# T

## The chip

a

## The reference

b

## The kernel before

c

## Time and profile before

d

### The profile page before, as it was taken

How to read it: one execution, taken by the hardware profiler on the slowest of the kernel's cores; microseconds unless marked ns; L12 is line 12 of the kernel's file. 1: busy time of each engine (PE TensorE's matmuls, PEld its weight loads, DVE VectorE, ACT ScalarE, POOL GpSimd, SP SyncE). 2: the span in 40 equal slices, each digit the busy share in tenths (PEclk: the TensorE clock that was granted, in tenths of full speed). 3: DMA queues.
4: the chain of work that ended last, by engine and by line, in shares of the span. 5: the costliest groups of instructions: out<-in, count | busy, mean ns of one | idle time of the engine just before them, and what ended most of it. 6: DMA issues, size and time to landing. Idle time of an engine off the chain costs nothing.

```text
span 3754.5 us, 41907 instructions; the slowest of 8 cores (3702.6 to 3754.5 us)
## 1 busy us (share of the span) xinstructions
PE 2815.8 (75%) x12672; PEld 1093.2 (29%) x12672; DVE 1725.6 (46%) x2582; ACT 752.6 (20%) x1317; POOL 292.3 (8%) x540
## 2 busy tenths in 40 slices
PE   0001787789977989689967988698869897899676
PEld 0000221323332333223322333233323333343222
DVE  2221555363645444463636454545455454736312
ACT  0000220304022220404022401322041304140201
POOL 0111000001000110001000110011000100110010
PEclk9999665879987899979987999789987999999878
DMA  6886000202230223213240233123321323122222
GB/s 197 241 242 172 12 4 20 62 23 71 85 101 29 57 82 88 75 31 89 67 112 17 63 96 87 48 57 85 96 68 40 92 78 90 52 84 73 90 79 84
DMA packets 108706, 303.98 MB, mean 81 GB/s; under 512 B 16192, under 2 KB 24768, under 8 KB 108496
## 3 DMA queue, kind: packets, MB, share of 16 engines
q1 hardware_dynamic: 61520, 169.14, 15.7%
q0 software_dynamic: 46976, 132.15, 12.6%
q8 instruction: 118, 1.93, 0.2%
q14 instruction: 92, 0.75, 0.1%
HBM read 269.77 MB, written 39.85 MB: 82 GB/s over the span
## 4 chain that ended last, share of the span: by engine, by line
PE 59%; DVE 12%; DMA 9%; issue 6%; ACT 4%; DVEq 0%; SPq 0%; ACTq 0%; POOLq 0%; POOL 0%
PE P L709 9%; PE P L440 9%; PE P L397 9%; PE P L387 8%; PE P L725 8%; PE P L622 6%; PE P L563 3%; DVE p_sb L674 3%; DMA wgb<-wg_s 3%; DMA wub<-wu_s 2%; PE P L763 2%; DMA wob<-wout_s 2%; DVE esum L648 2%; DMA wqb<-wq_s 2%; PE P L338 2%
## 5 line engine op out<-in xcount | busy, mean ns | idle before, releaser
L674 DVE TENSOR_TENSOR p_sb<-P,vdup 128x512 bf16<-128x512 f32 x1024 | 698.3, 689 | 387.5 <-PE P L725 351.2
L387 PE MATMUL P<-x_bf,wgb 128*128 128x512 bf16 x1536 | 526.4, 411 | 106.5 <-DMA wub<-wu_s 88.8
L709 PE MATMUL P<-e_sb,selz_sb 16*128 16x512 bf16 x1024 | 456.2, 455 | 130.9 <-DVE e_sb L658 77.3
L397 PE MATMUL P<-x_bf,wub 128*128 128x512 bf16 x1536 | 536.2, 409 | 7.4 <-DVE h_sb L413 7.3
L725 PE MATMUL P<-p_sb,id_sb 128*128 128x256 bf16 x2048 | 514.4, 317 | 35.1 <-DVE p_sb L674 31.2
L597 DVE TENSOR_TENSOR hadb<-q_sb,krep 128x2048 bf16<-128x2048 bf16 x256 | 309.9, 1224 | 470.1 <-PE P L622 310.2
L440 PE MATMUL P<-h_sb,wdb 128*128 128x512 bf16 x1536 | 481.9, 390 | 15.2 <-DVE r_bf L449 14.2
L622 PE MATMUL P<-hadb,selred_sb 128*16 128x256 bf16 x2048 | 324.5, 276 | 45.5 <-DVE hadb L597 21.4
L406 ACT ACTIVATE s_sil<-P 128x512 bf16<-128x512 f32 x192 | 114.4, 596 | 1052.0 <-PE P L387 1045.6
L305 PE MATMUL P<-x_bf,wd_sb 128*128 128x512 bf16 x128 | 35.4, 419 | 355.8 <-DMA x_bf<-xt 355.7
L763 PE MATMUL P<-avn,wob 128*128 128x256 bf16 x1024 | 249.5, 289 | 43.0 <-DMA wob<-wout_s 30.5
L413 DVE TENSOR_TENSOR h_sb<-s_sil,P 128x512 bf16<-128x512 bf16 x192 | 130.4, 679 | 305.4 <-PE P L397 230.8
L725 PEld LDWEIGHTS P<-p_sb,id_sb 128*128 128x128 bf16 x2048 | 170.5, 102 | 266.3 <-issue 232.8
L387 PEld LDWEIGHTS P<-x_bf,wgb 128*128 128x128 bf16 x1536 | 146.2, 101 | 317.8 <-issue 246.1
L709 PEld LDWEIGHTS P<-e_sb,selz_sb 16*128 16x128 bf16 x1024 | 91.9, 93 | 502.7 <-issue 502.7
L256 POOL DMA_DIRECT2D wgb<-wg_s x192 | 104.9, 547 | 1674.9 <-PE P L397 1674.2
L397 PEld LDWEIGHTS P<-x_bf,wub 128*128 128x128 bf16 x1536 | 153.5, 102 | 220.5 <-issue 134.0
L622 PEld LDWEIGHTS P<-hadb,selred_sb 128*16 128x16 bf16 x2048 | 153.4, 89 | 215.9 <-issue 192.5
L440 PEld LDWEIGHTS P<-h_sb,wdb 128*128 128x128 bf16 x1536 | 146.9, 99 | 203.0 <-issue 97.8
L338 PE MATMUL P<-x_bf,wqb 128*128 128x512 bf16 x512 | 138.2, 426 | 87.0 <-DMA wqb<-wq_s 75.7
L774 DVE SCALAR_TENSOR_TENSOR r_bf<-P,bout_sb,x_bf 128x256 bf16<-128x256 f32 x128 | 61.6, 482 | 246.6 <-PE P L763 246.6
L217 DVE CAST stgb<-stg 128x1024 bf16<-128x1024 int32 (+1 forms) x88 | 61.0, 694 | 226.2 <-DMA wg_s<-stgb 56.8
(65 smaller groups left out, 1933.0 us busy)
## 6 DMA issues: line engine op xcount, KB each, us to landing
wdb<-wdn_s SPq DMA_DIRECT2D x64, 768.0 KB, 4.5
wgb<-wg_s POOLq DMA_DIRECT2D x192, 256.0 KB, 3.0
wub<-wu_s POOLq DMA_DIRECT2D x192, 256.0 KB, 3.0
wob<-wout_s SPq DMA_DIRECT2D x128, 256.0 KB, 3.0
wqb<-wq_s SPq DMA_DIRECT2D x64, 256.0 KB, 3.0
yt<-x2b SPq DMA_DIRECT2D x64, 256.0 KB, 2.1
stg<-wg SPq DMA_DIRECT2D x24, 512.0 KB, 5.3
stg<-wu SPq DMA_DIRECT2D x24, 512.0 KB, 5.2
```

The source lines that it names most:

```text
L338: e.matmul(o, l, r, start=st, stop=sp)),
L387: e.matmul(o, l, r, start=st, stop=sp)),
L397: e.matmul(o, l, r, start=st, stop=sp)),
L406: e.activation(o, i, AF.Silu, scale=1.0 / 127.0)),
L413: h_v.append(add('V', (lambda e, o=o, a=a, b=b: e.tensor_mul(o, a, b)), waits=w, inc=s_v2, d=780))
L440: e.matmul(o, l, r, start=st, stop=sp)),
L597: add('V', (lambda e, o=o, a=q3, b=b: e.tensor_mul(o, a, b)), waits=tuple(w), inc=s_v, d=1460)
L622: e.matmul(o, l, r, start=st, stop=sp)),
L674: add('V', (lambda e, o=o, a=a, b=b: e.tensor_mul(o, a, b)), waits=w, inc=s_v, d=640)
L709: e.matmul(o, l, r, start=True, stop=True)),
L725: e.matmul(o, id_sb[:, :], r, start=st, stop=sp)),
L763: e.matmul(o, l, r, start=st, stop=sp)),
```

## The change

e

## Rows read from the trace of the kernel before

**Rows 1.** The page's first part, busy time by engine.
```profile
span 3754.5 us, 41907 instructions; the slowest of 8 cores (3702.6 to 3754.5 us)
...
PE 2815.8 (75%) x12672; PEld 1093.2 (29%) x12672; DVE 1725.6 (46%) x2582; ACT 752.6 (20%) x1317; POOL 292.3 (8%) x540
```

**Rows 2.** Windows, the six seams behind steps 1 to 6.
```profile
sum 129.00, PE 92.34 PEld 33.66 DVE 42.32 ACT 62.29 POOL 25.88; mean PE 15.39 PEld 5.61 DVE 7.05 ACT 10.38 POOL 4.31
```

**Rows 3.** Timeline behind step 5, and windows behind steps 5, 0 and 7.
```profile
2708.17 5.13 PE L440 MATMUL P<-h_sb,wdb 128*128 128x512 bf16 x23
...
2718.14 0.60 ACT L463 ACTIVATE musq<-P 128x512 f32<-128x512 f32 x1 [0.67 <-PE P L504]
...
2719.82 1.28 ACT L466 ACT_TABLE_LOAD   x1 [1.08 <-DVE vpe L472]
2721.12 0.72 ACT L466 ACTIVATE lnscr<-vpe,cvec_sb 128x512 f32<-128x512 f32 x1
...
2723.50 0.59 PE L846 MATMUL P<-r_bf,ones_sb 128*128 128x512 bf16 x1 [5.51 <-DVE nmb L477]
...
2723.50:2729.10 5.60, 5.30 (x17) 1.79 (x17) 4.77 (x7) 3.56 (x6) 0.00 (x0) 0.76 0.25 94
691.10:699.50 8.40, 5.81 (x18) 1.84 (x17) 4.93 (x8) 2.63 (x4) 1.08 (x2) 0.80 0.45 63
3502.90:3523.40 20.50, 4.97 (x18) 1.56 (x15) 17.21 (x28) 5.51 (x9) 0.00 (x0) 0.67 0.20 77
```

**Rows 4.** Windows, q projection of step 1, then steps 2 to 7.
```profile
700.50:720.20 19.70, 17.07 (x69) 6.71 (x70) 6.63 (x10) 4.81 (x7) 0.00 (x0) 0.90 0.37 107
...
sum 180.90, PE 108.28 PEld 40.30 DVE 96.01 ACT 28.86 POOL 0.00; mean PE 18.05 PEld 6.72 DVE 16.00 ACT 4.81 POOL 0.00
```

**Rows 5.** Timeline of step 3's q projection, SP's queue and PE.
```profile
1544.05 0.32 SPq L256 DMA_DIRECT2D wqb<-wq_s  x1
...
1552.77 0.58 PE L338 MATMUL P<-x_bf,wqb 128*128 128x512 bf16 x1 [5.89 <-DMA wqb<-wq_s]
```

**Rows 6.** Windows of AV0 (steps 5, 1 to 6, 7, 0), a block, and AV1.
```profile
2413.90:2497.60 83.70, 76.77 (x275) 22.41 (x276) 51.30 (x83) 2.98 (x5) 5.50 (x11) 0.72 0.12 32
...
sum 503.00, PE 460.82 PEld 136.53 DVE 308.46 ACT 17.91 POOL 32.86; mean PE 76.80 PEld 22.75 DVE 51.41 ACT 2.98 POOL 5.48
...
3209.90:3288.20 78.30, 75.08 (x330) 26.83 (x331) 53.98 (x87) 4.78 (x8) 9.84 (x18) 0.97 0.21 58
435.30:512.00 76.70, 66.48 (x186) 13.73 (x186) 48.24 (x77) 0.00 (x0) 0.00 (x0) 0.50 0.00 1
...
2447.10:2461.70 14.60, 14.52 (x43) 4.09 (x42) 6.50 (x10) 0.60 (x1) 1.09 (x2) 0.56 0.13 36
...
sum 474.80, PE 457.50 PEld 161.24 DVE 308.65 ACT 18.30 POOL 26.23; mean PE 76.25 PEld 26.87 DVE 51.44 ACT 3.05 POOL 4.37
```

**Rows 7.** Groups by line, and who waited for s_sil (us, times).
```profile
L709 PE MATMUL P<-e_sb,selz_sb 16*128 16x512 bf16 x1024 | 456.2, 455 | 130.9 <-DVE e_sb L658 77.3
...
L597 DVE TENSOR_TENSOR hadb<-q_sb,krep 128x2048 bf16<-128x2048 bf16 x256 | 309.9, 1224 | 470.1 <-PE P L622 310.2
...
L305 PE MATMUL P<-x_bf,wd_sb 128*128 128x512 bf16 x128 | 35.4, 419 | 355.8 <-DMA x_bf<-xt 355.7
...
  PE P L387: 1.3, 5
```

**Rows 8.** Windows, WO1 of step 0, then steps 1 to 6.
```profile
666.80:685.50 18.70, 13.59 (x65) 8.33 (x66) 3.38 (x7) 1.26 (x2) 0.00 (x0) 0.59 0.39 109
...
sum 157.30, PE 132.92 PEld 73.54 DVE 31.66 ACT 7.56 POOL 0.00; mean PE 22.15 PEld 12.26 DVE 5.28 ACT 1.26 POOL 0.00
```

**Rows 9.** Windows, WO0 and the stretch behind it, step 5.
```profile
2565.40:2601.90 36.50, 28.70 (x160) 14.89 (x160) 16.20 (x34) 4.87 (x7) 6.06 (x12) 1.00 0.51 144
```

**Rows 10.** Timeline of PE, first gate matmuls of the last FFN.
```profile
3523.37 3.15 PE L387 MATMUL P<-x_bf,wgb 128*128 128x512 bf16 x7 [15.03 <-DVE x2b L492]
```

More of the change, by code:

```diff
@@ L403, in plan_ffn_ch2 @@
                     w.append((s_v2, v0 + m - 1))
[L404 removed]
+                o, i_ = s_sil[m % 2][:, :], P[0 if m % 2 == 0 else 4][:, :]
                 add('S', (lambda e, o=o, i=i_:
@@ new lines, in plan_ffn_ch2 @@
+            for J in range(XC):
+                w = [(s_s2, sc2 + J + 1)]
+                if J == 0:
+                    w.append((s_s, ck['musq1']))
+                o2, r2 = P[3][:, :], sqb2[J % 2][:, :]
+                add('T', (lambda e, o=o2, r=r2, st=(J == 0), sp=(J == XC - 1):
+                          e.matmul(o, ones_sb[:, :], r, start=st, stop=sp)),
+                    waits=w, inc=s_pe2)
+            ex2_val = add('S', (lambda e, o=vpe2[:, :], i=P[3][:, :]:
+                                e.activation(o, i, AF.Identity,
+                                             scale=1.0 / 1024.0)),
+                          waits=[(s_pe2, pe2 + XC), (s_v2, ck['vpesub2'])],
+                          inc=s_s2)
```

208 lines of the change are left out of this document (122 added, 86 removed).

## The prediction

> **What bounds the kernel now.** I read the page's first part, then cut the span into the phases of a main step with the windows view, then the timeline at the places where PE stands still. PE is busy 75% of a 3754.5 us span and no other engine passes half [rows 1]; the first 345 us are weight preparation, which the change leaves alone. After that come eight steps of 512 tokens, and beside the attention of step s runs the feed-forward network (FFN) of step s-1, at places that the planner fixes when the program is built. So the question is not how busy PE is, but what each phase waits for.
>
> Between the last output-projection matmul of a step and the first head matmul of the next (the seam) lie 129.0 us over six steps, 21.5 each [rows 2]. In it PE does 23 left-over w_down matmuls, both LayerNorm statistics in turn, and stands 5.51 us in between, because the second statistics share P3 and P4 with the first and wait for nmb2 [rows 3]. The q projection behind it takes 180.9 us over steps 2 to 7, 30.2 each, and 19.7 in step 1, where no output is stored [rows 4]: SP issues in order, and by its order wqb loads stand behind yt stores that wait for x2b, and the last one behind two wdb loads, three times its size each, so that PE waits up to 5.89 us for one load, 8.7 us after its issue [rows 5]. The first attention-value phase of a step (AV0) takes 503.0 us over steps 1 to 6, 83.8 each, in step 5 at a mean granted clock of 0.72; in step 7 it takes 78.3 at 0.97 although it holds 150 FFN matmuls by the order and not 92, and in step 0 it takes 76.7 with none, at 0.50, the lower of the two levels, 1.2 GHz [rows 6]. So this phase is not limited by PE's work but by the ring PE, DVE, PE through two banks; FFN matmuls ride in it nearly free.
>
> **The change part by part.** The sum is made against the profiled execution, 3756.1 us. That is 0.85% above the median, 3724.24, so the result is scaled by 0.9915 at the end.
>
> The direct gains are small. The second gate bank P4 removes a wait of PE for the SiLU that is 1.3 us in the whole run, and the second x buffer a wait for x of 355.8 less the first 346.3, some 9.4 us, nearly all in step 1 [rows 7]. What counts is that the shorter dependences change the planner's order, as the rows of the order show, and that order is what I cost.
>
> Seam, steps 1 to 6. The w_down tail and all of the second LayerNorm's 16 matmuls move ahead of the end of the output projection. The seam is left with eight squares against ACT in lockstep, bounded by the old block of 16 (5.6 us [rows 3]; the pace is ACT's, so half the matmuls save nothing); then the eviction of E[x2] with Ln2 and its table load queued ahead of it on ACT, 1.28+0.72+0.60=2.6; then eight mean matmuls, 8 x 0.22=1.8 (0.22 is 5.13/23). Sum 10.0: 6 x 10=60 against 129.0, **-69**. Ends: 8 (if ACT reaches the eviction early) and 14 each, -81 to -45.
>
> Here a rule of the Trainium skill speaks against the change. Our rows have Ln starting 1.30 us after its table load begins [rows 3]. The page "ScalarE: Activation LUTs", section "What ACT_TABLE_LOAD costs", gives 1283 ns for the load and some 1380 ns more for a drain. By it a seam would be 1.4 us longer, some 8 us over six. The trace agrees on the load and shows no drain, so none is in the sum.
>
> q projection. SP's new order has all of wqb behind at most two yt, whose x2b is made before the head ends; the wdb pair stands behind. Six phases at 19.7 plus 1 us for the first gate matmul (below) are 124.2 against 180.9, **-57**. Ends: 19.7 gives -63; if half of the excess stays, -31.
>
> AV0. It now holds 139 FFN matmuls, 13 in the first of its eight blocks and 17 to 19 in the others, where before the first two blocks held 0 to 4. Its nearest row is step 7's 78.3. The one block in which the clock recovers under FFN work takes 14.6 instead of 9.6, an eighth of 76.7 [rows 6], and may now fall at the start. I take 80: 6 x 80=480 against 503.0, **-23**. Ends: 78.3, -33, and two such blocks on top of it, 88.3, +27.
>
> Second output projection (WO1), 157.3 over steps 1 to 6 [rows 8], 26.2 each, and I count step 7 the same, 183.5 in all. It holds 40 w_down matmuls and the 16 of the second statistics, not 87. Its first half stays at 3.2 us per group of 8; the second half is held by wob loads, 18.7/8=2.3 per group in step 0, where nothing else is there [rows 8]. 4 x 3.2+4 x 2.3=22, taken as 22.5, 157.5 over seven: **-26**. Ends: 18.7 each (-53) and no gain.
>
> First output projection with the stretch behind it, 36.5 us [rows 9], is held by the gate and up loads (95 gate and up matmuls, six pairs of loads). It now has 98 and five more of w_down: +1 each, **+7**, ends 0 and +18. AV1 loses 48 gate and up matmuls and gets 42 w_down; its 474.8 over six steps, 79.1 each [rows 6], stays.
>
> Seam behind step 0: statistics 5.6 become 8.1 (no Ln2 there), the head's 8.4 with its x waits [rows 3] become 3.6: **-2**.
>
> Last seam. Before, the first gate matmul of the last FFN starts 20.5 us behind WO1 and waits 15.03 us for the last x2b [rows 10]. It still has to, and the second LayerNorm's outputs are now begun only behind Ln2: nmb2 at about 8 us, then 32 DVE operations up to that x2b, at 28 in 20.5 us as before [rows 3], 23.4: 31.5, taken as 32.5, **+12**; ends 0 and +16. The last FFN itself keeps its loads and their order. Tail: means behind squares add an eviction, 8 matmuls and one more ACT pass, each with a hand-over: 0.9+1.9+0.9, **+4**, ends +2 and +5.
>
> -69-57-23-26+7-2+12+4=-154. 3756.1-154=3602, times 0.9915 is **3572 us**.
>
> **The rivals.** *The clock stays low in AV0 (slower).* PE still stands ahead of AV0 for the normalised e_sb [rows 7], and the 0.72 of today's phase says that its first half runs at the lower level. At that level 17 FFN matmuls of twice 0.22 on a ring of 9.6 make a block of up to 17; the one row for it, 14.6, had the clock back before its end [rows 6]. At 16 a phase is 128, +44 on the old one and +265 over six, against -131 from the other terms: 3890, scaled 3857. It decides where a phase passes 105.6 (+21.8), that is, from four or five such blocks of eight on. Against it: in step 5 the block behind the 14.6 is part of a phase that ends at full speed, and step 7 runs at 0.97. 6%.
>
> *The wait is only moved (no change).* The first gate matmul stands in PE's queue among the key and value projections, and needs the last x2b. I put that x2b at 41 us behind WO1: nmb2 at 9, then 34 DVE operations of 0.75 and two had of 1.22 [rows 7], and 4 for yt stores that have to land. PE comes there at 39 to 44: seam 10, head 4.7, q 20.6, key/value matmuls 4 to 9. If yt stores and had operations push it 15 us further, PE stands with everything behind it: +90, so -64, scaled 3661. 8%.
>
> *Only the direct waits go.* If phases are held by things that the reordering doesn't touch, 9.4+1.3=11 us stay: 3713. Against it: the q phase's excess is there by cause [rows 4, 5]. 6%.
>
> **How the numbers follow.** The forecast has 80%. A timing of this kernel can tell about 2% from no change, so faster means below 3650. All the good ends together give some -230, all the bad ones about -10, and neither is likely: I take -196 to -75, 3530 to 3650. What is left out below is the good ends, above the rivals. Faster 0.80, within 2% 0.15 (the second and third rival, and a little of the first), slower 0.05.
>
> **What would show it.** In the changed kernel's profile: seams of about 10 us; no PE wait over 3 us for wqb and q phases near 20; AV0 near 80 at a clock over 0.9; WO1 near 22; the last FFN starting some 32 us behind WO1; one Ln table load in front of L840's eviction. Wrong would be: AV0 above 90, PE waits of over 5 us at L395 for an x2b in every step, or a seam that is still 20 us.

## The result, and the profile after

The change takes the kernel from 3725.6 to **3674.6 us** (medians of 6 and 7 runs), a ratio of **0.9858** with a 95% interval of 0.9839 to 0.9878: 1.4% faster, clear of noise but below the 2% from which the prediction counted a change as faster. The forecast was 3572 us with a range of 3530 to 3650. The direction was right, the size was not: 51 us of the 152 that it forecast. In some runs of any of these kernels one die shows a lower granted clock and the time is up to some per cent longer; medians are over all runs, ratios and intervals over the others alone.

The sections ahead of the prediction on the chip, the reference, the kernel before, its time and the change hold single letters in place of text. The description stands at the end of this document, under "The kernel and the change", and was not on record with the prediction; a reader who is new to the kernel should take it first.

The page of the changed kernel (its first part and the row of the granted clock, in tenths per fortieth of the span):

```profile
span 3671.2 us, 41956 instructions; the slowest of 8 cores (3639.1 to 3671.2 us)
...
PE 2758.6 (75%) x12672; PEld 1090.5 (30%) x12672; DVE 1725.1 (47%) x2582; ACT 774.0 (21%) x1349; POOL 292.5 (8%) x540
...
PEclk9999756689998999999989999998999998999778
```

The profiled execution took 3673.0 us, within 0.05% of the median. That of before was 0.85% above the median of its first two runs. The views of the cores, before and then after, show why: before, one die had a lower granted clock than the other, and the slowest core, of which every row ahead of the prediction is one, lies on it.

```profile
core 0: 3754.5 us, clock 0.880
die 0 (median of its cores): 3746.3 us, clock 0.884
die 1 (median of its cores): 3712.4 us, clock 0.898
```

```profile
core 7: 3671.2 us, clock 0.901
die 0 (median of its cores): 3648.1 us, clock 0.909
die 1 (median of its cores): 3663.9 us, clock 0.903
```

The clock records of the traces say what the lower mean is made of. Beside 1.00 (2.4 GHz) and 0.50 (1.2 GHz) they hold stretches at a granted 0.81: 235 to 274 us in all on each of cores 0 to 3 of before and none on its cores 4 to 7; none in x_two_old_order (below), and in the changed kernel 27 to 59 us on each of cores 4 to 7 alone.

So core 0 of before is a poor base for the phases in which the clock matters. For the balance I use the mean of eight cores, and as base a kernel that differs from before only in having two x buffers under the same order (x_two_old_order, below: ratio 1.0012), whose execution shows no such die.

The windows that answer to [rows 2], [rows 4], [rows 6] and [rows 8], slowest core of the changed kernel, cut at the same matmuls: the six seams, q of steps 2 to 7, AV0, WO1 and AV1 of steps 1 to 6:

```profile
sum 62.50, PE 38.89 PEld 12.18 DVE 16.90 ACT 45.27 POOL 3.23; mean PE 6.48 PEld 2.03 DVE 2.82 ACT 7.55 POOL 0.54
...
sum 129.80, PE 94.70 PEld 36.24 DVE 89.49 ACT 28.95 POOL 0.00; mean PE 15.78 PEld 6.04 DVE 14.92 ACT 4.82 POOL 0.00
...
sum 484.50, PE 446.69 PEld 158.66 DVE 321.06 ACT 28.71 POOL 52.44; mean PE 74.45 PEld 26.44 DVE 53.51 ACT 4.78 POOL 8.74
...
sum 142.90, PE 123.58 PEld 68.04 DVE 28.07 ACT 34.23 POOL 18.35; mean PE 20.60 PEld 11.34 DVE 4.68 ACT 5.71 POOL 3.06
...
sum 483.10, PE 460.70 PEld 160.34 DVE 301.46 ACT 7.58 POOL 10.20; mean PE 76.78 PEld 26.72 DVE 50.24 ACT 1.26 POOL 1.70
```

The seams fall from 129.0 to 62.5 (10.4 each, forecast 10.0), q from 180.9 to 129.8 (forecast 124.2). WO1 goes from 157.3 to 142.9, AV0 from 503.0 to 484.5, and AV1 rises from 474.8 to 483.1.

In this table a phase lasts from its first matmul to the first of the next, summed over the eight steps and averaged over the eight cores of one execution each, in us. "Last" is all behind the last WO1.

| phase | base | x_two | stats_one_bank | gate_one_bank | changed | before_costs | combined |
|---|---|---|---|---|---|---|---|
| seams | 133 | 51 | 133 | 72 | 70 | 66 | 72 |
| head | 50 | 51 | 54 | 55 | 55 | 54 | 55 |
| q | 223 | 209 | 164 | 168 | 170 | 198 | 164 |
| KV0 and SC0 | 323 | 322 | 330 | 327 | 327 | 324 | 329 |
| gap ahead of AV0 | 75 | 75 | 75 | 75 | 75 | 75 | 75 |
| AV0 | 665 | 667 | 673 | 671 | 671 | 699 | 644 |
| KV1 and SC1 | 499 | 509 | 507 | 502 | 501 | 493 | 499 |
| WO0 and the stretch behind | 297 | 312 | 304 | 326 | 326 | 298 | 283 |
| AV1 | 644 | 649 | 687 | 632 | 657 | 702 | 635 |
| WO1 | 197 | 183 | 190 | 185 | 184 | 186 | 181 |
| last | 252 | 256 | 266 | 267 | 272 | 268 | 207 |
| span, with what lies ahead of step 0 | 3704 | 3628 | 3726 | 3623 | 3655 | 3706 | 3489 |
| median of the runs | 3727.9 | 3651.7 | 3753.9 | 3644.1 | 3674.6 | 3726.0 | 3503.4 |

(before_costs is not quite the changed kernel at the old costs; see there.)

The changed kernel wins 115 us in the seams and q, and 13 in WO1. It gives back 29 in WO0 and the stretch behind it, 14 in AV1, 6 in AV0, 20 behind the last WO1 and 10 in small pieces. That makes -49, and the medians say -51.

### The profile page after: what moved, and what is told of

Read it like the earlier page. It is cut to its first block, busy times and chain, and to the rows that moved or that the text cites. A ratio compares the mean times of both kernels' runs of the same rounds, so it can differ in the third digit from the quotient of the medians.

```text
span 3671.2 us, 41956 instructions; the slowest of 8 cores (3639.1 to 3671.2 us)
## 1 busy us (share of the span) xinstructions
PE 2758.6 (75%) x12672; PEld 1090.5 (30%) x12672; DVE 1725.1 (47%) x2582; ACT 774.0 (21%) x1349; POOL 292.5 (8%) x540
## 4 chain that ended last, share of the span: by engine, by line
PE 60%; DVE 9%; DMA 9%; issue 6%; ACT 4%; DVEq 0%; ACTq 0%; POOLq 0%; SPq 0%; POOL 0%
PE P L448 10%; PE P L405 9%; PE P L731 9%; PE P L395 9%; PE P L747 8%; PE P L644 7%; PE P L585 3%; DVE p_sb L696 3%; DMA wgb<-wg_s 3%; DMA wub<-wu_s 3%; PE P L344 2%; PE P L785 2%; DVE esum L670 2%; DMA wqb<-wq_s 2%; DMA wob<-wout_s 1%
## 5 line engine op out<-in xcount | busy, mean ns | idle before, releaser
L395 PE MATMUL P<-x_bf,wgb 128*128 128x512 bf16 x1536 | 519.9, 407 | 110.5 <-DMA wub<-wu_s 90.2
L405 PE MATMUL P<-x_bf,wub 128*128 128x512 bf16 x1536 | 518.2, 406 | 19.1 <-DVE h_sb L421 19.1
L731 PE MATMUL P<-e_sb,selz_sb 16*128 16x512 bf16 x1024 | 427.9, 425 | 131.7 <-DVE e_sb L680 68.5
L448 PE MATMUL P<-h_sb,wdb 128*128 128x512 bf16 x1536 | 504.9, 393 | 17.1 <-DVE r_bf L457 16.4
L747 PE MATMUL P<-p_sb,id_sb 128*128 128x256 bf16 x2048 | 496.4, 300 | 23.9 <-DVE p_sb L696 17.7
L644 PE MATMUL P<-hadb,selred_sb 128*16 128x256 bf16 x2048 | 321.8, 276 | 43.0 <-DVE hadb L619 20.4
L311 PE MATMUL P<-x_bf,wd_sb 128*128 128x512 bf16 x128 | 36.4, 434 | 354.1 <-DMA x_bf<-xt 353.9
L785 PE MATMUL P<-avn,wob 128*128 128x256 bf16 x1024 | 235.1, 292 | 43.4 <-DMA wob<-wout_s 29.0
L747 PEld LDWEIGHTS P<-p_sb,id_sb 128*128 128x128 bf16 x2048 | 177.7, 101 | 223.4 <-issue 173.4
L395 PEld LDWEIGHTS P<-x_bf,wgb 128*128 128x128 bf16 x1536 | 150.8, 102 | 307.7 <-issue 225.8
L731 PEld LDWEIGHTS P<-e_sb,selz_sb 16*128 16x128 bf16 x1024 | 91.9, 92 | 489.4 <-issue 488.4
L261 POOL DMA_DIRECT2D wgb<-wg_s x192 | 104.9, 546 | 1558.4 <-PE P L405 1550.6
L405 PEld LDWEIGHTS P<-x_bf,wub 128*128 128x128 bf16 x1536 | 150.6, 102 | 222.5 <-issue 138.6
L644 PEld LDWEIGHTS P<-hadb,selred_sb 128*16 128x16 bf16 x2048 | 151.8, 89 | 211.8 <-issue 189.0
L448 PEld LDWEIGHTS P<-h_sb,wdb 128*128 128x128 bf16 x1536 | 144.0, 99 | 213.6 <-issue 126.3
L344 PE MATMUL P<-x_bf,wqb 128*128 128x512 bf16 x512 | 127.3, 400 | 53.9 <-DMA wqb<-wq_s 38.3
```

What stands on the lines that cost most here:

```text
L344: e.matmul(o, l, r, start=st, stop=sp)),
L395: e.matmul(o, l, r, start=st, stop=sp)),
L405: e.matmul(o, l, r, start=st, stop=sp)),
L448: e.matmul(o, l, r, start=st, stop=sp)),
L644: e.matmul(o, l, r, start=st, stop=sp)),
L731: e.matmul(o, l, r, start=True, stop=True)),
```

## The experiments

They ran in four groups, each with runs of the kernel before on the same chip. First, the parts of the change, alone and left out.

**x_two_old_order.** The kernel before with the two x buffers. The waits of before stay visible to the planner and are not carried out (`pw`), so every engine's order is the old one.

```diff
+                if c == 0 and ck['kv_pe_end']:
+                    pw.append((s_pe, ck['kv_pe_end']))
+                pw.append((s_v, max(ck['wo0_list'][c], ck['wo1_list'][c])))
+                w.append((s_v, ck['wo_free'][s % 2][c]))
...
-            for sem, val in nd[0]:
+            for sem, val in nd[0] + PW[id(nd)]:
```

> The kernel before with two x buffers, the planner still seeing the old waits, so that every engine's order is that of before. If the change works through the order (theory 'order'), only the x waits go, nearly all in step 1: -5 to -10 us of 3725, and the seams stay at 21.5 and q at 30. If the removed wait itself matters (theory 'direct waits'), -30 us or more and head or q phases shorter in every step.

3727.9 us, ratio 1.0012 (0.9998 to 1.0026). The buffer by itself is worth nothing that the time shows. The q phases keep their 223 us, and the head loses 5 (55 in before, by the same mean over eight cores).

**x_two.** The same buffers, with the planner seeing the new waits.

> The same two x buffers, now seen by the planner. By the order it moves 47 FFN matmuls into AV0 and leaves 41 w_down matmuls in WO1 and none in the seam; LayerNorm statistics stay on two banks in turn. Theory 'order': seam down from 21.5 to about 15, AV0 at 84 with 139 FFN matmuls, total 3685 to 3705. Theory 'direct waits': the same time as with the old order, within 5 us.

3651.7 us, ratio 0.9803 (0.9785 to 0.9821). The same buffer gives 76 us once the order may change, more than either theory said. Its seams are 51 us in the table, 7 each, although both LayerNorms still take P3 and P4 in turn: the order alone puts the w_down tail and the second LayerNorm ahead. The forecast had named the sharing of P3 and P4 as what holds the seam, and had not split the gain between the parts of the change. This one part is also faster than the whole change (0.9803 against 0.9858, intervals apart).

**stats_one_bank.** The changed kernel with one x buffer and gate on P0: only the statistics and the costs.

```diff
-        x_bf = [E(nc.sbuf_tensor(f"x_bf{i}", ...)) for i in range(2)]
+        x_bf = [E(nc.sbuf_tensor("x_bf", [128, XC * ST], BF16))] * 2
...
+                if c == 0 and ck['kv_pe_end']:
+                    w.append((s_pe, ck['kv_pe_end']))
-                wfree = ck['wo_free'][s % 2]
+                wfree = ck['wo_free'][0]
```

> The changed kernel with one x buffer and gate on P0 alone: the LayerNorm statistics on one bank and the stated costs are all that is left of the change. Theory 'the statistics carry it': seams near 11 and q near 22, so -100 us there, and part of it is given back in WO0 and AV1, in all 3670 to 3690, as good as the whole change. Theory 'x carries it': 3700 or more, with seams at 16 or above.

3753.9 us, ratio 1.0073 (1.0047 to 1.0100): slower than before. Seams stay at 133, q falls to 164, and AV1 rises to 687; in this order it holds 40 gate and up and 119 w_down matmuls. The second theory held: without the second x buffer there is no gain in the seams or in the time. But q falls by 59 us with one x buffer, so q's gain comes with the statistics and the costs, which no run here tells apart.

**gate_one_bank.** The changed kernel with gate on P0 alone.

```diff
-                    w.append((s_s2, sc0 + m - 1))
+                    w.append((s_s2, sc0 + m))
-                    o = P[0 if m % 2 == 0 else 4][:, :]
+                    o = P[0][:, :]
```

> The changed kernel with gate on P0 alone. Its order has the same numbers of FFN matmuls by phase as the changed kernel. The wait for SiLU was 1.3 us in the whole run before, so 3675 within 8 us if the second gate bank is worth nothing; 3690 or more if DVE and ACT hold PE in gate groups now that more of them lie in AV0.

3644.1 us, ratio 0.9777 (0.9754 to 0.9799): the second gate bank makes the change 30 us worse. By the table it is AV1, 632 against 657; everything else is within 6 us. **gate_two_banks_one_bank_order** asks whether it is the bank or its order: gate on P0 and P4, SiLU waits for the group before visible to the planner alone.

> The changed kernel with gate on P0 and P4 as it stands, but every engine's order that of gate_one_bank (the planner sees the wait for the SiLU of the group before). If the 30 us between gate_one_bank (3644) and the changed kernel (3675) are the order's, this takes 3635 to 3655 and AV1 is at 632 per core, not 657. If the second bank itself costs (theory 'bank'), 3670 or more.

AV1 is at 633.5 us per core, and the mean core took 3616 us, against 3623 for gate_one_bank and 3655 for the changed kernel. So the profile puts it on the order. Of its four runs (3639.7, 3663.7, 3671.9 and 3690.7 us) only the first can enter a ratio; it lies in the 3635 to 3655 expected, but one run has no interval, and by the times alone the question would stay open.

**before_costs.** This was meant as the changed kernel with the planner's costs as they were (700 for Square, 510 for x1). Its edit does more: it also raises the cost of the 1024 products `p_sb` of the AV blocks, which is 640 in both kernels, to 830.

```diff
-                    waits=w, inc=s_s2, d=850)
+                    waits=w, inc=s_s2)
...
-                            waits=w, inc=s_v, d=640)
+                            waits=w, inc=s_v, d=830)
```

> The changed kernel with the planner's costs as they were in the kernel before. By the order 40 gate and up matmuls stay in AV1 and AV0 holds 100, not 137. Theory 'costs are a small part': 3665 to 3690. Rival 'costs carry the x gain': 3700 or more, with seams over 15 us.

3726.0 us, ratio 0.997 (0.994 to 1.0001): some 1% slower than the changed kernel, for the same instructions with the same waits, so the planner's figures alone move the time by as much as the change does. The seams are short (66 us), yet the order leaves 41 gate and up matmuls and 149 w_down in AV1 and 100 in AV0. On its slowest core AV0 and AV1 take 515.8 and 519.0 us over steps 1 to 6, against 484.5 and 483.1 in the changed kernel.

The time is as the second theory said, its seams of over 15 us are not (9.5 each). What the change's own cost figures are worth stays open: the AV blocks, where most of the loss lies, are the place whose planned cost the edit also raised. That the gain of x doesn't need the new figures is shown by x_two, which has the old ones.

**The short waits of PE.** In the changed kernel the second block of AV1 begins like this (timeline of PE in step 5):

```profile
2535.31 0.38 PE L747 MATMUL P<-p_sb,id_sb 128*128 128x256 bf16 x2 [0.58 <-DVE p_sb L696]
2535.62 0.60 PE L731 MATMUL P<-e_sb,selz_sb 16*128 16x512 bf16 x2
2537.03 0.38 PE L448 MATMUL P<-h_sb,wdb 128*128 128x512 bf16 x1 [0.81 <-DVE r_bf L457]
2537.63 0.58 PE L731 MATMUL P<-e_sb,selz_sb 16*128 16x512 bf16 x1 [0.22 <-DVE p_sb L696]
2538.15 0.61 PE L448 MATMUL P<-h_sb,wdb 128*128 128x512 bf16 x1
```

The windows of AV1's first three blocks there; the clock is the number behind the five engines:

```profile
2525.60:2536.30 10.70, 10.01 (x46) 3.49 (x45) 7.20 (x13) 0.00 (x0) 1.67 (x4) 1.00 0.32 85
2536.30:2551.00 14.70, 13.66 (x43) 4.33 (x43) 6.36 (x10) 0.63 (x1) 0.00 (x0) 0.65 0.16 64
2551.00:2560.50 9.50, 9.11 (x42) 3.17 (x42) 6.37 (x10) 0.63 (x1) 0.00 (x0) 1.00 0.26 85
```

PE stands 0.58 us for `p_sb`, does four short matmuls, stands 0.81 us for the residual of the w_down group before and another 0.22 for `p_sb`, and then matmuls take 0.6 us where they took 0.38: the granted clock is at the lower level, 1.2 GHz, and the block takes 14.7 us, not 9.5 to 10.7. In 8 cores and 7 steps of the changed kernel, such a spell starts at this place in 50 AV1 phases of 56; it lasts 3.4 to 13.7 us. In gate_one_bank's steps 1 and 3 the same pauses stand there, and 14 phases of 16 have it. In its steps 2 and 4 to 7 four w_down matmuls stand in place of the wait of 0.81 us, only the 0.58 is left, and every one of those 40 phases is at a clock of 1.00 (timeline of PE, step 4):

```profile
2130.10 0.60 PE L729 MATMUL P<-e_sb,selz_sb 16*128 16x512 bf16 x2
2130.64 1.04 PE L446 MATMUL P<-h_sb,wdb 128*128 128x512 bf16 x4
2131.61 0.39 PE L729 MATMUL P<-e_sb,selz_sb 16*128 16x512 bf16 x1
```

The windows of its AV1, steps 1 to 6 together:

```profile
sum 463.40, PE 444.52 PEld 157.76 DVE 302.15 ACT 7.55 POOL 10.22; mean PE 74.09 PEld 26.29 DVE 50.36 ACT 1.26 POOL 1.70
```

That is 463.4 us against 483.1. Nor is a wait of 0.81 us enough by itself: in step 6 of gate_one_bank one stands 49 us into AV1, on all eight cores, and no spell follows.

**down_two_banks** takes the wait away by giving w_down P2 and P4 in turn, the order kept.

```diff
-                if mo >= 1:
-                    w.append((s_v2, v1 + mo))
+                if mo >= 2:
+                    w.append((s_v2, v1 + mo - 1))
-                    o = P[2][:, :]
+                    o = P[2 if mo % 2 == 0 else 4][:, :]
```

> The changed kernel, every engine's order kept, with w_down groups on P2 and P4 in turn, so that the first matmul of a group no longer waits for the residual of the group before. In AV1 that wait, 0.8 us at the start of a block, stands right ahead of most spells at half clock, each worth 4 to 5 us. If the wait seeds them (theory 'pause'), AV1 falls from 657 us per core (all eight steps) to 630 to 640 and the ratio to before from 0.986 to about 0.980. If the spells come from how densely FFN matmuls lie in the block (theory 'density'), AV1 stays within 5 us of 657.

3648.1 us, ratio 0.9811 (0.9763 to 0.9859), but not by what I expected: AV1 stays at 655 (657). The trace of its step 4 shows why. The w_down matmul no longer waits, and the `e_sb` matmul behind it waits 1.1 us, since DVE has the residual and the copy of `avn` ahead of its next `p_sb`. The longer pause was moved by one instruction, not removed (42 phases of 56 still have the spell), so this run could not tell the two theories apart. The time came from WO0 (-4), q (-5) and the last FFN (-9), in one execution each.

**fill_av1** fills the pause instead: four matmuls whose result nothing reads.

```diff
+                        if hf == 1 and s >= 1 and J in (1, 5) and (kind, idx2) == ('b', 2):
+                            for i in range(4):
+                                add('T', (lambda e: e.matmul(
+                                    P[1][:, :], ones_sb[:, :], wd_sb[:, 0:512],
+                                    start=True, stop=True)), waits=(), d=0)
```

> The changed kernel, its order kept, with 4 matmuls that nothing reads ahead of the third e_sb matmul of AV1's second and sixth block, in steps 1 to 7, where PE pauses 0.5 to 0.8 us. Theory 'pause': AV1 falls from 657 us per core to 632 to 642, its clock from 0.90 to 0.92 or more, as in gate_one_bank whose order has no pause there. Rival: the spells come from the rest of the order; AV1 stays at 652 to 662.

3651.2 us, ratio 0.9767 (0.9688 to 0.9847), the interval wide because the runs of before scattered in this group. AV1 falls to 639.6 per core, and on four of the eight cores every AV1 of steps 1 to 7 is at 78.9 to 79.9 us and a clock of 1.00. The block's start (timeline of PE, core 4, step 4; L714 are the fills):

```profile
2111.07 0.60 PE L736 MATMUL P<-e_sb,selz_sb 16*128 16x512 bf16 x2
2111.60 1.04 PE L714 MATMUL P<-wd_sb,ones_sb 128*128 128x512 bf16 x4
2112.48 0.38 PE L448 MATMUL P<-h_sb,wdb 128*128 128x512 bf16 x1
```

The windows of AV1, steps 1 to 6, slowest core:

```profile
sum 465.80, PE 450.13 PEld 160.42 DVE 301.49 ACT 7.55 POOL 10.29; mean PE 75.02 PEld 26.74 DVE 50.25 ACT 1.26 POOL 1.71
```

465.8 against 483.1, with eight matmuls more in each AV1. Behind the filled place no spell starts, in any of the 56 phases. So the pause seeds the spell. On the other four cores, 0 to 3, all of one die, eight phases are still longer. That is something else: most of their lost clock is at 0.81 and not at 0.50, it comes at any place, and two cores have it in the same steps (windows of core 3 and core 4, step 7):

```profile
3304.70:3331.20 26.50, 26.13 (x103) 8.70 (x104) 15.28 (x24) 0.00 (x0) 0.00 (x0) 0.81 0.20 61
3304.70:3331.20 26.50, 25.19 (x119) 10.07 (x122) 15.12 (x24) 0.61 (x1) 0.00 (x0) 1.00 0.19 60
```

What grants 0.81 to one die, in one execution and not in the next, no run here shows.

**fill_before_av0.** The same idea for AV0, with 24 matmuls in the wait for the normalised `e_sb`.

> The changed kernel with 24 matmuls of 128x512 that nothing reads, put into the 9.4 us in which PE waits for the normalised e_sb ahead of AV0, in steps 1 to 7; the order is otherwise the same. If AV0's first block takes 16.7 us because the clock is at half level (forecast's step 'AV0 at 80' failed by that), it falls to 11 and AV0 from 671 to about 635 per core, total near 3640. If the block is long for another reason, AV0 stays and the total rises by 0 to 10.

A miss: 3664.3 and 3695.8 us in the two of five runs that enter the ratio, 0.9884 (0.9816 to 0.9952). The mean core took 3653 us (3655 without), AV0 669.7 (671.0). The gap's clock rose from 0.81 to 0.95 over the eight steps (to 1.00 in steps 1 to 7, which have the fills), and yet the first block is at half level, because a second wait stands inside it. In the changed kernel (timeline of PE, step 5):

```profile
2324.00 1.89 PE L395 MATMUL P<-x_bf,wgb 128*128 128x512 bf16 x8
2332.55 1.10 PE L731 MATMUL P<-e_sb,selz_sb 16*128 16x512 bf16 x2 [6.66 <-DVE e_sb L680]
2336.97 0.58 PE L731 MATMUL P<-e_sb,selz_sb 16*128 16x512 bf16 x1 [3.33 <-DVE p_sb L696]
```

The windows of AV0's first two blocks there:

```profile
2332.60:2347.60 15.00, 11.15 (x38) 3.41 (x38) 9.80 (x18) 0.00 (x0) 0.55 (x1) 0.66 0.06 18
2347.60:2357.30 9.70, 9.25 (x43) 3.32 (x42) 6.35 (x10) 0.60 (x1) 1.09 (x2) 1.00 0.19 56
```

PE waits 6.66 us, does two `e_sb` matmuls, and waits 3.33 more for the first `p_sb`, since DVE normalises all eight pieces of `e_sb` first (4.03 us). The first block takes 15.0 us at 0.66. **fill_before_and_in_av0** puts 14 more matmuls there:

```diff
+                        if hf == 0 and s >= 1 and J == 0 and (kind, idx2) == ('b', 2):
+                            for i in range(14):
+                                add('T', ... )     # as above, into P7
```

> As fill_before_av0, with 14 more matmuls that nothing reads between the second and the third e_sb matmul of AV0's first block, where PE stands 3.1 to 3.3 us for the first p_sb. Theory 'pause': with both waits filled the clock stays up, the first block falls from 16.7 (16.1 with the first fill alone) to 11 to 12, AV0 from 671 to 630 to 640 per core. Rival: the spell at half clock comes at that place with PE busy too, AV0 stays at 665 to 675.

3635.7 us, ratio 0.9737 (0.9712 to 0.9762). AV0 falls from 671.0 to 645.3 per core at a clock of 0.93. Windows of steps 1 to 6, slowest core:

```profile
sum 467.40, PE 444.68 PEld 162.76 DVE 320.31 ACT 30.92 POOL 52.45; mean PE 74.11 PEld 27.13 DVE 53.39 ACT 5.15 POOL 8.74
```

467.4 against 484.5. It is 645 and not the 630 to 640 expected: the first block still takes 13.5 us (core 3, step 4), since the fills don't shorten the waits.

**The serial loads.** The window of WO0 in step 5 of the changed kernel:

```profile
2480.40:2511.10 30.70, 24.39 (x123) 13.11 (x124) 6.02 (x11) 3.08 (x4) 4.37 (x8) 0.83 0.41 120
```

The timeline of PE in it:

```profile
2486.20 0.82 PE L785 MATMUL P<-avn,wob 128*128 128x256 bf16 x6
2490.77 1.87 PE L395 MATMUL P<-x_bf,wgb 128*128 128x512 bf16 x4 [3.75 <-DMA wub<-wu_s]
2492.65 0.63 PE L395 MATMUL P<-x_bf,wgb 128*128 128x512 bf16 x1
```

POOL's queue beside it:

```profile
2481.70 0.55 POOL L261 DMA_DIRECT2D wgb<-wg_s  x1 [5.99 <-PE P L405]
2486.25 0.55 POOL L261 DMA_DIRECT2D wub<-wu_s  x1 [4.00 <-DMA wgb<-wg_s]
2486.90 0.55 POOL L261 DMA_DIRECT2D wgb<-wg_s  x1
2492.47 0.55 POOL L261 DMA_DIRECT2D wub<-wu_s  x1 [5.02 <-DMA wgb<-wg_s]
```

PE waits 3.75 us for an up load, and then runs at the lower level (0.63 for a matmul). The up load was issued at 2492.47 only when its gate load had landed, since `dma()` lets two loads on one semaphore go one after the other. The Trainium skill ("DMA: Bandwidth & Descriptors", "Why a DMA increments its semaphore by 16 and not by 1") says why such a wait is needed: of two DMAs in flight on one semaphore, the count for the first can be reached before all its data is there, and a semaphore for each buffer in flight ends that. No run here shows it. The clock was 1.00 in [rows 9], over WO0 and the stretch behind it, and is 0.83 in this WO0. **up_load_own_semaphore** gives the up loads two semaphores of their own, the order kept.

```diff
-                dma('G', s_gd[m % 2], d2, r2s)
+                dma('G', s_gu[m % 2], d2, r2s, pw=[(s_gd[m % 2], s_gd[m % 2].c)])
...
-                w = [(s_gd[m % 2], gd0[m % 2] + 32 * (m // 2 + 1))]
+                w = [(s_gd[m % 2], gd0[m % 2] + 16 * (m // 2 + 1))]
...
-                w2 = []
+                w2 = [(s_gu[m % 2], gu0[m % 2] + 16 * (m // 2 + 1))]
```

> The changed kernel, every engine's order kept, with the up loads on semaphores of their own: an up load is issued at once behind its gate load and doesn't wait for that to land, and a gate group waits for its own load alone. Theory 'serial loads': the PE waits for wub (40 us in WO0, 19 behind it, 50 in the last FFN) go and with them WO0's spells at a lower clock: 3590 to 3615. Rival, 'the loads are bound by bandwidth': the two land together after 4.5 us or more, half of the waits stays: 3640 to 3655.

3551.4 us, ratio 0.9534 (0.9503 to 0.9566): more than twice what the whole change gave, and below my range. The waits of the gate matmuls on loads (us, times), changed kernel, then this one:

```profile
  DMA wub<-wu_s: 90.2, 33
```

```profile
  DVE x2b L534: 20.1, 1
  DMA wgb<-wg_s: 5.8, 12
```

POOL now issues the two 0.53 us apart, and both land as fast as before (the page's DMA part, median us from issue to landing in the last column; before and changed kernel: 3.0 and 3.0):

```profile
2487.50 0.55 POOL L265 DMA_DIRECT2D wgb<-wg_s  x1 [10.55 <-PE P L412]
2488.03 0.55 POOL L265 DMA_DIRECT2D wub<-wu_s  x1
```

```profile
wgb<-wg_s POOLq DMA_DIRECT2D x192, 256.0 KB, 3.0
wub<-wu_s POOLq DMA_DIRECT2D x192, 256.0 KB, 3.1
```

WO0 falls from 211 to 174 per core and the part behind the last WO1 from 272 to 205. The rival with bandwidth is out. In WO0 and behind it, steps 1 to 7, the time at the lower clock falls from 44 to 22 us per core. The kernel before had 88.8 us of such waits in its trace too; I had read them and left them out, because the change doesn't touch them.

**last_ffn_early.** In addition the first gate group waits for the product and SiLU of the FFN before, not its last `x2b`. In the changed kernel it waits 19.73 us, 31.9 us behind the last WO1:

```profile
3411.20 3.54 PE L850 MATMUL P<-r_bf,ones_sb 128*128 128x512 bf16 x8 [0.89 <-ACT vpe L840]
3434.47 3.57 PE L395 MATMUL P<-x_bf,wgb 128*128 128x512 bf16 x8 [19.73 <-DVE x2b L527]
```

> The same as up_load_own_semaphore, and the first gate group of an FFN waits for the product and SiLU of the FFN before, not for its last x2b and Exp; order kept. In the changed kernel it waits 19.7 us for x2b in the last FFN. If that wait is all that holds it, another -15 to -20 us; if x1, made by the same DVE behind the x2b operations, comes as late, 0 to -5.

Nothing by the ratio: 0.9538 (0.9489 to 0.9586) against 0.9534, the last part 207 us against 205. The first gate matmul starts 18.6 us behind WO1, but each one then waits for its piece of x1, which DVE makes in turn with the `x2b` operations:

```profile
3351.80 0.58 PE L400 MATMUL P<-x_bf,wgb 128*128 128x512 bf16 x1 [6.48 <-DVE x_bf L897]
3354.20 0.59 PE L400 MATMUL P<-x_bf,wgb 128*128 128x512 bf16 x1 [1.82 <-DVE x_bf L897]
```

**Adding up.** **gate_one_bank_up_own** and **x_two_up_own** carry the up loads' semaphores to two other orders.

> gate_one_bank with its order, and the up loads on semaphores of their own. If the two are independent, 3644 less the 120 us that the same edit took from the changed kernel: 3515 to 3535. If the clean order of AV1 is lost with the new timing, 3545 to 3555.

> x_two (the kernel before with two x buffers, statistics on two banks) with its order, and the up loads on semaphores of their own: 3652 less 110 to 120 us if independent, 3530 to 3545. It tells whether the statistics on one bank are worth having beside it.

3533.3 us, ratio 0.9464 (0.9439 to 0.9488), and 3557.8 us, ratio 0.9518 (0.9489 to 0.9547). The first adds as expected. The second took 94 us from x_two, by the medians and by the mean core, and not 110 to 120. So the statistics on one bank together with the cost figures, beside two x buffers and the loads' repair, are worth some 20 us (24 by the medians, 17 by the mean core); the intervals of the two ratios nearly touch.

**combined** is gate_one_bank_up_own with all three fills.

> gate_one_bank_up_own (3533) with the fills before and in AV0 and in AV1's second and sixth block, order kept. AV0's fill took 25 us per core from the changed kernel; AV1 has spells in steps 1 and 3 alone, some 8 us. If they add up: 3495 to 3510.

3503.4 us, ratio 0.9387 (0.9321 to 0.9453), the best of all, 4.7% below the changed kernel. All 56 of its AV1 phases in steps 1 to 7 are at a clock of 1.00.

## Why the prediction was wrong

The forecast's terms against the table (base to changed; the terms for the first and last seam are put to their phases):

| step of the sum | forecast | measured |
|---|---|---|
| seams, the one behind step 0 included | -71 | -62 |
| q projection | -57 | -53 |
| AV0 | -23 | +6 |
| WO1 | -26 | -14 |
| WO0 and the stretch behind | +7 | +29 |
| AV1 | 0 | +14 |
| last seam and tail | +16 | +20 |
| all else (head, key/value, SC) | 0 | +10 |
| sum | -154 | -49 |

Of the 105 us that are missing, three steps of the sum make 65: AV0 29, WO0 22 and AV1 14. WO1 makes 12, the seams 9, and 10 lie in phases that the sum left at nothing. The signs that the prediction named for its own success nearly all came: seams of 10.4 us, no wait over 3.0 us for `wqb`, AV0 at 80.8 us and a clock of 0.91 (steps 1 to 7), the last FFN 31.9 us behind WO1, one table load in front of L840. None of them looked at WO0 or AV1, or at the base. The range was cut too narrow as well: the bad ends of its own terms came to -10, AV1 had no ends at all, and WO0 ended above its bad end (+29 against +18).

- **Seam and q: right in size, and by the mechanism named, the order.** 10.4 us per seam, and q at 21.6, with no wait over 3.0 us for `wqb` (7.1 before). The part behind it was not what the reading of the seam suggests: its gain belongs to the order that two x buffers allow (x_two: 51 us). The statistics on one bank and the cost figures together cost 20 us there and give 39 in q (x_two 209, gate_one_bank 168 to 170).
- **"AV0. I take 80": the level was right, the gain failed.** 484.5 over six steps is 80.8. The price of a block with FFN matmuls at full clock was right, 9.5 to 10, and 47 matmuls more did ride in the phase nearly free. The forecast's "may now fall at the start" did happen, in each of the five steps that I cut into blocks on core 7: 13 FFN matmuls in the first block, most of it at half clock, 15 to 17 us (12 to 14 in x_two_old_order on its core 7). What failed is the term subtracted. 83.8 per step is core 0's, on the die with the stretches at 0.81. Counted up to the next phase, steps 1 to 6 take 519.1 us on that core, 503.0 on the base's slowest core and 501.1 on the changed kernel's. The fall from 503.0 to 484.5 between [rows 6] and the windows after looks like the forecast and is mostly the core's. The rival "the clock stays low in AV0" named the right cause in the wrong size: it is one block of eight.
- **"First output projection: +1 each": failed by 22 us.** I counted eight matmuls more and put each at its own time, though the working said that loads hold the phase. The loads alone are not what grew. On core 7, steps 1 to 7, WO0 and the stretch behind it wait 46 us for `wub` in x_two_old_order and 42 in the changed kernel; in the changed kernel 40 of them lie in WO0 itself, in 15 longer waits, where there were 19 in 20. What grew is the wait for the product `h_sb`, from 8 to 19 us, the wait for `e_sb`, from 3.5 to 8.4, and, over the eight cores, the time at the lower clock, from 15 to 44 us each. The waits of the whole run on core 7, x_two_old_order and then the changed kernel, whose 90.2 us for `wub` are shown above (us in total, times, longest):

```profile
PE P L396 <- DMA wub<-wu_s: 91.8, 49, 4.7
PE P L406 <- DVE h_sb L422: 7.9, 8, 1.4
```

```profile
PE P L405 <- DVE h_sb L421: 19.1, 8, 3.1
```

up_load_own_semaphore takes 39 us from this row and halves its time at the lower clock, so the longer waits for loads carry part of that; which of the rest seeds what stays open.

- **"AV1 ... stays": failed.** The number of FFN matmuls hardly changes (153 to 147), but where w_down groups begin in a block does. Two pauses of 0.58 and 0.81 us at the start of the second block bring a spell at half clock that costs up to 5 us. gate_one_bank and fill_av1 show it.
- **WO1: right sign, half the size.** 23.8 per step on the slowest core, not 22.5. The base was 4 us too high as well: 183.5 us in the sum, 179 over steps 1 to 7 for the mean core of x_two_old_order.
- **Last seam and tail: right.** Gate starts 31.9 us behind WO1, forecast 31.5 to 32.5.
- **"Only the direct waits go", 11 us:** the direct effect of x, most of it, is 0 in the time (x_two_old_order), so even this floor was too high.

On the table load, the trace after agrees with that of before: Ln starts 1.30 us after its load begins, and the load begins within 0.1 us of the end of what it stands behind, so the drain that the Trainium skill adds ("ScalarE: Activation LUTs", "What ACT_TABLE_LOAD costs") did not show, and the seam came out at 10.4.

## What to carry to other kernels

In a kernel whose order is planned, a dependence that is removed is worth what the planner makes of it: cost the order, and freeze it in an experiment before crediting the edit. Where moved work lands, ask which wait it lands behind, and look for pauses of PE under one microsecond that stand close together: they cost far more than their length when the clock falls behind them. Signs of success have to cover every term of the sum, the base too. Check that an edit for an experiment touches nothing else. Take the base of a clock-bound phase from several cores, and read what makes a load late even when the change doesn't touch it: here two loads on one semaphore, 90 us of waits, were worth more than the change.

## What the runs showed of the hardware

- Two pauses of PE, of 0.58 and 0.81 us and under 2 us apart, in otherwise dense work are followed by a spell at 1.2 GHz in 50 AV1 phases of 56; it lengthens a block from 9.5 or 10 to as much as 14.8 us. Either pause alone is followed by none (gate_one_bank, 40 phases with the first, 8 with the second). Four matmuls that nobody reads in place of the second leave no spell there in 56 phases (AV1, 657 to 640 us per core).
- Filling only the first of two waits did nothing for the phase (AV0 670 against 671): the gap's clock rose to 1.00, and fell behind the second wait of 3.1 to 3.3 us. Filling both gave 26 us.
- Two loads of 256 KB issued 0.5 us apart landed after 3.0 and 3.1 us, no later than one alone.
- Cores of one execution that run the same program differed by 32 us (changed kernel) to 52 us (before). The difference goes with the mean granted clock, 0.880 to 0.898 in before, and there with stretches at a granted 0.81 on the four cores of one die, 235 to 274 us on each.

## The kernel and the change

**The chip, the cores and the metric.** The kernel runs on all 8 cores of one Trainium2 chip. The cores share nothing in the computation: each takes 4096 of the 32768 tokens and a copy of the weights. The metric is the device time in microseconds of the slowest core, as the median over runs. Engines are named as the profile names them: PE (matmul), PEld (weight load of PE), DVE (vector), ACT (scalar), POOL and SP. Here the last two do nothing in the main part but issue DMAs.

**The reference.** The inputs are x of shape (4, 8192, 1024) and one layer's weights; H = 16 heads of 64.

```python
q = x @ Wq + bq
kv = (x @ Wdown + bdown) @ Wup + bup           # latent of 256
q, k, v = ...                                  # (B, T, 16, 64), rope on q and k
att = softmax(einsum('bthd,btgd->bthg', q, k) / sqrt(64))
out = einsum('bthg,btgd->bthd', att, v).reshape(B, T, D) @ Wout + bout
x = layernorm(x + out)
h = silu(x @ wg.T) * (x @ wu.T)                # hidden 3072, w = int / 127
x = layernorm(x + h @ wd.T)
```

The attention is over the 16 heads of one token, not over tokens. Both LayerNorms have no scale and no shift. A token's q and k are rotated by the same angle, so their product doesn't depend on it, and the kernel leaves the rotation out.

**The kernel before.**

**Layout.** Activations are kept transposed, features on the 128 partitions and tokens along the free axis, x coming in as `xt` [1024, 4096]. A core works in eight steps of 512 tokens (ST), and a step's attention in two halves (`hf`) of 256 tokens. The first part of the program brings the weights in, casts them to bf16 and writes those of wq, wout, gate, up and down back to DRAM. In every step they are streamed again as `wqb`, `wob`, `wgb`, `wub` (128x1024) and `wdb` (128x3072), each in two buffers.

**A step's attention** (channel `m` of the planner) has these phases:

- head (`plan_head`): x arrives in `x_bf` in eight DMAs on POOL's queue, 16 matmuls give the latent (L305). Then eight groups of eight matmuls on `wqb` give q (L338). SP issues the `wqb` loads.
- KV of a half (`plan_kv_part`): keys and values from the latent (L563), evicted by ACT to `krep` and `vdup`.
- SC of a half (`plan_sc`): for each head g DVE forms `hadb` = q * k_g over all 16 heads (L597), PE sums it over the 64 channels with `selred_sb` (L622), ACT takes the exponential into `e_sb`.
- AV of a half (`plan_av`): DVE sums and normalises `e_sb` (L648, L658). Then come eight blocks (J). In each block PE spreads `e_sb` over the partitions with `selz_sb` (L709, 8 matmuls) into P5 and P6 in turn, DVE multiplies with `vdup` into `p_sb` (L674), and PE sums these with the identity into P7 (L725, 16 matmuls), which DVE copies to `avn`.
- WO of a half (`plan_wo`): eight groups of eight matmuls on `wob` (L763). DVE adds the bias and x (L774), which gives `r_bf` (`r1_bf` in the code).

The order in a step is KV, SC, AV of half 0 (AV0), KV and SC of half 1, WO of half 0 (WO0), AV of half 1 (AV1), WO of half 1 (WO1). Then come the first LayerNorm's statistics (16 matmuls with `ones_sb`: sums of r in P3, sums of squares in P4, L846 and L850, the squares by ACT), `nmb`, and 16 DVE operations that write `x1_bf`, the FFN's input.

**The feed-forward network (FFN)** of step s-1 (`plan_ffn_ch2`, channel `c`) is planned beside the attention of step s. It has 24 gate groups of eight matmuls in P0 (L387) and as many up groups in P1 (L397), SiLU by ACT (L406), the product by DVE into `h_sb` (L413); then eight w_down groups of 24 matmuls in P2 (L440), residual by DVE (L449), and the second LayerNorm: statistics in the same banks P3 and P4 (L500, L504), musq2 (L463), vpe2 (L472), Ln and Exp (L466, L469), `nmb2` (L477). Last, each of eight blocks takes a product (L486) and a sum `x2b` (L492), and SP stores `x2b` to `yt`. POOL issues the gate and up loads, SP the `wdb` loads. The tile names in the trace drop their numbers, and some tiles show another buffer's name at the same form: gate and up matmuls read as `P<-x_bf,wgb`, both residuals as `r_bf`, both `vpe` as `vpe`.

**What sets the order.** No engine picks work at run time. `add(stream, fn, waits, inc, n, d)` records an instruction with the semaphore values it waits for and an estimated cost `d` in ns (default by engine, `DDEF`). At the end a list scheduler merges the two channels of every engine into one fixed order: again and again it takes, of the heads of all channels, the one with the smallest key of estimated start (in bins of 800 ns), then the longest path to the end:

```python
key = (round(es / 800.0), -CP[id(nd)], es)
```

Within a channel the order stays as it was written. The semaphore values are then renumbered to the merged order, and each engine runs its list, waiting in front of an instruction where needed. SP's and POOL's lists are merged by the same rule, so a load behind a store in SP's list is issued only when the store's data is ready. `dma()` adds a wait for the previous DMA on the same semaphore.

The waits that matter here: the loads of x wait for WO1's L774 of the previous step, since that still reads `x_bf` (L283). A gate group m waits for the SiLU of group m-1 (L379). The first statistics matmul of one LayerNorm waits for the other's `musq` and `vpe`, because they share P3 and P4. The first gate matmul of an FFN waits for the last DVE operation of the FFN before, its last `x2b` (L376).

**Time and profile before.**

| what | value |
|---|---|
| time, median of 2 runs | 3724.24 us (3723.25 to 3725.23) |
| the profiled execution | 3756.08 us |
| its span (the rows' time base) | 3754.5 us, cores 3702.6 to 3754.5 us |
| busy: PE, DVE, ACT, POOL | 75%, 46%, 20%, 8% |
| mean granted PE clock, core 0 | 0.880 |

The page and the trace are of one execution, on the slowest of its cores, so durations taken from it belong to 3756.08 us and not to the median. A window row gives the stretch, its length, each engine's busy time in the order PE, PEld, DVE, ACT, POOL with its number of instructions, then the granted PE clock as a share of full speed, the share of time that the DMA engines were busy, and GB/s. In rows of groups and of the timeline, the number in brackets or behind the bar is idle time of the engine just before the instruction, and behind `<-` stands what ended it.

**The change.** It has four parts.

1. `x_bf` becomes two buffers, taken in turn by step. The loads of x wait for the last reader of the same buffer two steps ago (`ck['wo_free']`), and the wait for the key and value matmuls of the previous step at the first load goes.
2. The gate groups use P0 and P4 in turn, and group m waits for the SiLU of group m-2.
3. Each LayerNorm's statistics use P3 alone. First come the eight squares matmuls, then ACT copies their sum over 1024 to `vpe`, then the eight matmuls of the means into the same bank, and ACT copies them over 1024 to `meanb1` or `meanb2` (new). Square, a subtraction by DVE (`tensor_sub`, both operands in SBUF), Ln and Exp follow, and `nmb` is formed from `meanb` and not from PSUM. A LayerNorm's first statistics matmul now waits only for the other's copy of the means (`ck['musq1']`, `ck['musq2']`), no longer for the other's `vpe`. The instructions of the squares and of the means are written down ahead of the `x2b` and `x1` operations, where they stood behind them before.
4. Some estimated costs of the planner are stated: 850 for Square (700 before), 640 for the subtraction, 830 for `nmb` and for the 16 operations of `x1` (510 before).

The rest doesn't bear on the device: an unused tile goes, a line prints the free memory if an environment variable is set, and the planner's error message is longer.

```diff
@@ plan_head
+            xb = x_bf[s % 2]
...
-                if c == 0:
-                    if ck['kv_pe_end']:
-                        w.append((s_pe, ck['kv_pe_end']))
-                if ck['wo_stt_end']:
-                    w.append((s_v, max(ck['wo0_list'][c], ck['wo1_list'][c])))
+                wfree = ck['wo_free'][s % 2]
+                if wfree is not None:
+                    w.append((s_v, wfree[c]))
@@ plan_ffn_ch2, gate
+                elif m == 1:
+                    w.append((s_s2, s_b2))
                 else:
-                    w.append((s_s2, sc0 + m))
+                    w.append((s_s2, sc0 + m - 1))
                 for c in range(XC):
-                    o = P[0][:, :]
+                    o = P[0 if m % 2 == 0 else 4][:, :]
@@ plan_ffn_ch2, second LayerNorm (the first is changed alike)
             for J in range(XC):
                 w = [(s_v2, r2_v[J])]
                 if J >= 2:
-                    w.append((s_pe2, pe2 + 2 * (J - 1)))
+                    w.append((s_pe2, pe2 + J - 1))
...
-                waits=[(s_pe2, pe2 + 2 * XC), (s_s, ck['musq1'])], inc=s_s2)
+                    waits=w, inc=s_s2, d=850)
+            for J in range(XC):
+                w = [(s_s2, sc2 + J + 1)]
+                if J == 0:
+                    w.append((s_s, ck['musq1']))
+                o2, r2 = P[3][:, :], sqb2[J % 2][:, :]
...
+            ex2_val = add('S', (lambda e, o=vpe2[:, :], i=P[3][:, :]:
+                                e.activation(o, i, AF.Identity,
+                                             scale=1.0 / 1024.0)),
+                          waits=[(s_pe2, pe2 + XC), (s_v2, ck['vpesub2'])],
+                          inc=s_s2)
+            for J in range(XC):
+                w = [(s_v2, r2_v[J])]
+                if J == 0:
+                    w.append((s_s2, ex2_val))
+                o, r = P[3][:, :], r2_bf[:, J * ST:(J + 1) * ST]
...
+            mean2_val = add('S', (lambda e, o=meanb2[:, :], i=P[3][:, :]:
+                                  e.activation(o, i, AF.Identity,
+                                               scale=1.0 / 1024.0)),
+                            waits=[(s_pe2, pe2 + 2 * XC), (s_v2, ck['nmb2_v'])],
+                            inc=s_s2)
+            musq_val = add('S', (lambda e, o=musq2[:, :], i=meanb2[:, :]:
+                                 e.activation(o, i, AF.Square)),
+                           waits=[(s_s2, mean2_val)], inc=s_s2)
+            vpe2_val = add('V', (lambda e, o=vpe2[:, :], a=vpe2[:, :],
+                                 b=musq2[:, :]: e.tensor_sub(o, a, b)),
+                           waits=[(s_s2, musq_val), (s_v2, s_v2.c)],
+                           inc=s_v2, d=640)
...
-                if J == 0:
-                    w += [(s_s, ck['musq1']), (s_v, ck['nm1'])]
...
-            ck['musq2'] = musq_val
-            ck['vpe2'] = v2 + 2
+            ck['musq2'] = mean2_val
```

In the changed kernel the lines lie elsewhere: x load L291, latent L311, q L344, gate L395, up L405, w_down L448, second LayerNorm's squares L475 and means L488, SC L644, AV L731 and L747, WO L785, first LayerNorm's squares L837 and means L850; `dma()` is L261, where it was L256.

The planner sees other waits and costs, so the order of the instructions changes in many places. Three of them follow.

PE, end of step 4 up to the head of step 5, before. L440 and L763 are w_down and WO1, L500 and L504 the second LayerNorm's sums, L846 and L850 the first's, L305 the next step's latent:

```order
L440 MATMUL P<-h_sb,wdb 128x512
L763 MATMUL P<-avn,wob 128x256
L440 MATMUL P<-h_sb,wdb 128x512 x23
L500 MATMUL P<-r_bf,ones_sb 128x512
L504 MATMUL P<-sqb,ones_sb 128x512
...
L846 MATMUL P<-r_bf,ones_sb 128x512
L850 MATMUL P<-sqb,ones_sb 128x512
...
L305 MATMUL P<-x_bf,wd_sb 128x512 x16
```

The same place after the change:

```order
L785 MATMUL P<-avn,wob 128x256
L475 MATMUL P<-sqb,ones_sb 128x512
L785 MATMUL P<-avn,wob 128x256 x4
...
L475 MATMUL P<-sqb,ones_sb 128x512
L785 MATMUL P<-avn,wob 128x256 x4
L488 MATMUL P<-r_bf,ones_sb 128x512
L785 MATMUL P<-avn,wob 128x256
...
L837 MATMUL P<-sqb,ones_sb 128x512 x8
L850 MATMUL P<-r_bf,ones_sb 128x512 x8
L311 MATMUL P<-x_bf,wd_sb 128x512 x16
```

The w_down matmuls are done before WO1's last groups, the second LayerNorm's 16 sums lie among WO1's groups, and only the first LayerNorm's 16 stand between WO1 and the head, the squares ahead of the means.

PE, end of half 0's SC and first block of AV0 in step 5, before (L622 is SC, L387 and L397 are gate and up, L709 and L725 AV):

```order
L622 MATMUL P<-hadb,selred_sb 16x256 x8
L387 MATMUL P<-x_bf,wgb 128x512 x4
L709 MATMUL P<-e_sb,selz_sb 128x512 x3
L725 MATMUL P<-p_sb,id_sb 128x256 x2
L709 MATMUL P<-e_sb,selz_sb 128x512
...
L725 MATMUL P<-p_sb,id_sb 128x256 x6
L709 MATMUL P<-e_sb,selz_sb 128x512 x2
L397 MATMUL P<-x_bf,wub 128x512 x4
L709 MATMUL P<-e_sb,selz_sb 128x512
```

After:

```order
L644 MATMUL P<-hadb,selred_sb 16x256 x16
L405 MATMUL P<-x_bf,wub 128x512 x4
L395 MATMUL P<-x_bf,wgb 128x512 x8
L731 MATMUL P<-e_sb,selz_sb 128x512 x3
L747 MATMUL P<-p_sb,id_sb 128x256 x2
L405 MATMUL P<-x_bf,wub 128x512
L731 MATMUL P<-e_sb,selz_sb 128x512
L405 MATMUL P<-x_bf,wub 128x512
L747 MATMUL P<-p_sb,id_sb 128x256
L405 MATMUL P<-x_bf,wub 128x512
L747 MATMUL P<-p_sb,id_sb 128x256
```

Before, four gate matmuls stood ahead of the first block, none in it, and four up matmuls behind the first instructions of the second. Now twelve stand ahead of the first block, and up matmuls lie singly between its instructions.

SP's queue around the head of step 3, before (all by `dma()`):

```order
L256 DMA wqb<-wq_s 128x1024 x2
L256 DMA yt<-x2b 128x512 x4
L256 DMA wqb<-wq_s 128x1024 x3
L256 DMA yt<-x2b 128x512
L256 DMA wqb<-wq_s 128x1024
...
L256 DMA yt<-x2b 128x512
L256 DMA wdb<-wdn_s 128x3072 x2
L256 DMA wqb<-wq_s 128x1024
```

After:

```order
L261 DMA wqb<-wq_s 128x1024 x2
L261 DMA yt<-x2b 128x512
L261 DMA wqb<-wq_s 128x1024 x6
L261 DMA yt<-x2b 128x512
L261 DMA wob<-wout_s 128x1024
L261 DMA yt<-x2b 128x512
L261 DMA wob<-wout_s 128x1024
L261 DMA yt<-x2b 128x512 x5
L261 DMA wdb<-wdn_s 128x3072 x2
```

Before, stores of `x2b` lay between the `wqb` loads, and two `wdb` loads stood ahead of the last of them. After, one store stands ahead of the last six `wqb` loads, and the other stores and the `wdb` pair behind them.
